# Moving the small product of the softmax sums and their reciprocals from VectorE to GpSimd

## The reference, cut to what matters

```python
def attention(x, w_in, b_in, w_out, b_out):          # x: 8 x 512 x 256, 16 heads of 16
    x_proj = (x @ w_in.T + b_in).reshape(b, l, h, -1)
    q, k, v = jnp.split(x_proj, 3, axis=-1)
    att = jnp.einsum('blhd,bmhd->blmh', q, k) * scale
    att = jax.nn.softmax(att, axis=2)
    opt = jnp.einsum('blmh,blhd->blhd', att, v).reshape(b, l, d)
    return opt @ w_out.T + b_out

x = x + layernorm(attention(layernorm(x)))
x = x + layernorm(feed_forward(layernorm(x)))
```

## Time and profile before

| | |
|---|---|
| median of three runs | 537.91 us (537.71 to 538.23) |
| the profiled execution's own time | 539.01 us |
| its span, first to last instruction | 537.2 us |
| PE busy | 512.8 us (95%) |
| DVE busy | 473.9 us (88%) |
| ACT busy | 453.8 us (84%) |
| POOL busy | 344.9 us (64%) |
| granted TensorE clock, mean | 0.997 of full speed |

### The profile page before, as it was taken

One profiled execution on the slowest core, in us unless ns is written; L12 is line 12 of the kernel. 1 busy time (PEld: TensorE's weight loads), 2 busy tenths in 40 slices (PEclk: granted clock), 3 DMA queues, 4 the chain that ended last, 5 costly groups with the idle time before them and its releaser, 6 DMA issues.

```text
span 537.2 us, 8929 instructions
## 1 busy us (share of the span) xinstructions
PE 512.8 (95%) x2752; PEld 410.2 (76%) x2752; DVE 473.9 (88%) x1005; ACT 453.8 (84%) x1238; POOL 344.9 (64%) x544
## 2 busy tenths in 40 slices
PE   8999989999999999999999999999999999999995
PEld 6746555688898769876897779876897777678995
DVE  4598999988999899998999899999999899995455
ACT  3599998999899998999899998999899988895230
POOL 5697047415973788539972798449971888497462
PEclk9999999999999999999999999999999999999998
DMA  6694353026220635036230625035310760210011
GB/s 215 205 224 131 95 142 78 2 51 168 53 82 2 157 80 156 2 78 158 60 99 1 163 74 157 1 97 138 80 39 6 177 171 1 65 54 1 1 40 40
DMA packets 22691, 47.63 MB, mean 89 GB/s; under 512 B 5266, under 2 KB 13586, under 8 KB 22004
## 3 DMA queue, kind: packets, MB, share of 16 engines
q1 hardware_dynamic: 21956, 45.95, 32.5%
q10 hardware_dynamic: 432, 0.59, 0.4%
q0 software_dynamic: 256, 0.52, 0.4%
HBM read 8.24 MB, written 4.19 MB: 23 GB/s over the span
## 4 chain that ended last, share of the span: by engine, by line
PE 42%; ACT 35%; DVE 9%; SPq 4%; issue 3%; POOL 3%; DMA 1%; POOLq 0%; ACTq 0%
ACT ps L523 26%; PE pu L199 20%; PE ps L227 8%; PE pu L283 4%; PE ps L199 3%; DVE nmax L735 3%; SPq L1199 3%; ACT qk L537 3%; PE pu L239 2%; PE ps L206 2%; DVE st L777 2%; ACT y L590 2%; DMA stack<-qk 1%; ACT vo L545 1%; POOL y L1029 1%
## 5 line engine op out<-in xcount | busy, mean ns | idle before, releaser
L523 ACT ACTIVATE ps<-ps,nmax 128x512 f32<-128x512 f32 x512 | 348.9, 721 | 19.2 <-DVE nmax L735 18.3
L735 DVE TENSOR_REDUCE nmax<-ps 128x1 f32<-128x512 f32 x512 | 322.3, 680 | 17.4 <-PE ps L227 16.8
L227 PE MATMUL ps<-stack 128*128 128x512 f32 x512 | 184.6, 418 | 3.9 <-ACT ps L523 3.2
L523 ACT ACTIVATION_READ_ACCUMULATOR ps<-ps,nmax 128x1 f32 x512 | 137.6, 269 | 0.0
L227 PEld LDWEIGHTS ps<-stack 128*128 128x128 f32 x512 | 93.5, 189 | 33.5 <-ACT ps L523 20.9
L199 PEld LDWEIGHTS pu<-wo_r,inter 128*128 128x128 f32 x696 | 88.3, 188 | 2.8
L199 PE MATMUL pu<-wo_r,inter 128*128 128x256 f32 x696 | 90.4, 282 | 0.0
L199 PE MATMUL pu<-yT,wi_r 128*128 128x512 f32 x336 | 87.4, 395 | 0.4 <-ACT xn L590 0.4
L199 PEld LDWEIGHTS pu<-yT,wi_r 128*128 128x128 f32 x336 | 63.1, 189 | 14.1 <-ACT xn L590 0.7
L206 PE MATMUL ps<-ones_r 128*128 128x512 f32 x132 | 55.3, 461 | 6.2 <-ACT ps L523 5.1
L206 PEld LDWEIGHTS ps<-ones_r 128*128 128x128 f32 x132 | 25.9, 199 | 32.4 <-ACT ps L523 26.2
(11 more groups left out here) (154 smaller groups left out, 701.5 us busy)
## 6 DMA issues: line engine op xcount, KB each, us to landing
stack<-qk SPq DMA_DIRECT2D x256, 128.0 KB, 2.5
xb<-in_x SPq DMA_DIRECT2D x7, 512.0 KB, 3.7
out_y<-xb SPq DMA_DIRECT2D x7, 512.0 KB, 3.6
xb<-in_wo SPq DMA_DIRECT2D x1, 1024.0 KB, 7.8
vo<-in_wi SPq DMA_DIRECT2D x2, 512.0 KB, 7.0
oT<-in_wqk ACTq DMA_DIRECT2D x1, 512.0 KB, 4.9
xb<-in_x SPq DMA_DIRECT2D x4, 128.0 KB, 4.8
stack<-qk SPq DMA_DIRECT2D x8, 64.0 KB, 2.5
```

What stands on the lines that cost most here:

```text
L227: e.matmul(ps[i % NS][:], st[:, 1 - p, c, t * 128:(t + 1) * 128], st[:, 2, c, :], start=True, stop=True).then_inc(scored, 1)
L523: e.activation(ps[i % NS][:], ps[i % NS][:], ACT.Exp, bias=nmax[:, i % 8:i % 8 + 1], accum_out=ssum[:, b % 2, t, h:h + 1]).then_inc(exped, 1)
L735: e.tensor_reduce(nmax[:, i % 8:i % 8 + 1], ps[i % NS][:], AX_X, ALU.max, negate=True).then_inc(maxed, 1)
```

## The change

The product that makes `sone` is taken out of VectorE's `ratio` and `ratio_half` and put at the head of GpSimd's `scale` and `scale_half`, behind their waits. VectorE now signals a new semaphore `inverted` after the reciprocal, GpSimd waits for it, multiplies, signals `ratioed` and waits for its own signal before it scales. The counts of `ratioed` are halved where they are waited for.

```diff
@@ scalar, exponential @@
                 if b >= 2 and k == 0:
-                    e.wait_ge(ratioed, 2 * (b - 2) + 2)
+                    e.wait_ge(ratioed, b - 1)
@@ vector, ratio @@
                     if b:
                         e.wait_ge(scaled, 4 * b)
-                    e.reciprocal(srec[:], ssum[:, b % 2]).then_inc(ratioed, 1)
-                    e.wait_ge(ratioed, 2 * b + 1)
-                    e.tensor_tensor(sone[:], ssum[:, b % 2], srec[:], ALU.mult).then_inc(ratioed, 1)
+                    e.reciprocal(srec[:], ssum[:, b % 2]).then_inc(inverted, 1)
@@ vector, ratio_half @@
-                e.reciprocal(srec[:, ts], ssum[:, b % 2, ts]).then_inc(ratioed, 1)
-                e.wait_ge(ratioed, 2 * (b + h) + 1)
-                e.tensor_tensor(sone[:, ts], ssum[:, b % 2, ts], srec[:, ts], ALU.mult).then_inc(ratioed, 1)
+                e.reciprocal(srec[:, ts], ssum[:, b % 2, ts]).then_inc(inverted, 1)
@@ pool, scale @@
                     e.wait_ge(v_whole, 4 * b + 4)
-                    e.wait_ge(ratioed, 2 * b + 2)
+                    if b:
+                        e.wait_ge(scaled, 4 * b)
+                    e.wait_ge(inverted, b + 1)
+                    e.tensor_tensor(sone[:], ssum[:, b % 2], srec[:], ALU.mult).then_inc(ratioed, 1)
+                    e.wait_ge(ratioed, b + 1)
                     scale_tiles(b, ALL)
@@ pool, scale_half @@
-                e.wait_ge(ratioed, 2 * (b + h) + 2)
+                ts = slice(2 * h, 2 * h + 2)
+                e.wait_ge(scaled, 4 * b)
+                e.wait_ge(inverted, b + h + 1)
+                e.tensor_tensor(sone[:, ts], ssum[:, b % 2, ts], srec[:, ts], ALU.mult).then_inc(ratioed, 1)
+                e.wait_ge(ratioed, b + h + 1)
                 scale_tiles(b, HALVES[h])
```

More of the change, by code:

```diff
@@ L117, in sandwich @@
         scored, maxed, exped = sem("scored"), sem("maxed"), sem("exped")
-        ratioed, scaled = sem("ratioed"), sem("scaled")
+        inverted, ratioed, scaled = sem("inverted"), sem("ratioed"), sem("scaled")
         xnT_ps, qk_ps, v_ps, oT_ps, y_ps, yT_ps = (sem(n + "_ps") for n in ("xnT", "qk", "v", "oT", "y", "yT"))
```

## The result

Over 15 runs each, the changed kernel takes 536.75 us (536.47 to 538.28) and the kernel before 537.81 us: a ratio of 0.9983, with a 95% interval of 0.9976 to 0.9990. That is 0.9 to 1.1 us less, where the prediction said 0.4 less and a range of 535.2 to 538.8. The verdict "same", which the prediction drew at 0.2% or 1.08 us, holds, by the medians with 0.02 us to spare. But the interval doesn't reach 1: it is a small gain, and more than twice the size that was forecast.

A forecast was written before the change was run, and what follows sets the result against it. The period was taken to close over GpSimd (ScalarE, copy, subtraction, scaling, transposes, projection), with the held product beside it. The terms sum to 7p - 2.73 = -0.4 us, from 537.91 to 537.5 us, range 535.2 to 538.8.

The forecast's parts named there:

- The hold: VectorE's product at five changes of sequence waits about 1.5 us until GpSimd's long subtraction ends; it is not slow itself.
- The chain's 1.35 us: "Issue" time of VectorE's product in the chain of waits; claimed no measure of gain, as the period closes over GpSimd.
- VectorE is the bound: Rival: VectorE sets the pace, so five holds of 1.64 us go: -8.2 us, 529.7 us; chance 0.08.
- both of TensorE's waits go: Rival: at four steady changes TensorE's waits of 0.41 and 0.27 us vanish: -2.7 us, 535.2 us; chance 0.10.
- The four steady changes: Changes near 191, 250.8, 310.6 and 370.4 us: scaling later, second transposes no longer wait; p - 0.50 each.
- p: Time of the product on GpSimd, taken as 0.33 us from a plain two-input operation of 128 x 64.
- d: How much later GpSimd's scaling starts at a steady change: p - 0.07, or 0.26 us.
- The seventh change: Change into the last sequence: ScalarE's copy, late before from VectorE's stall, then follows the transposes; p - 0.35.
- The first change and the last half: Places without a hold, where TensorE waits for the scaling, so its delay is paid: p - 0.19 each.
- The second change: Scaling ends at 135.50, TensorE needs it at 136.10; 0.46 us cover the delay, so it costs nothing.
- The queue behind the product: GpSimd's later copy, subtraction and norms, delayed 0.26 us, hidden by TensorE's work; uncovered, 1.0 us over four periods.
- The slower rival: Product dear on GpSimd, delaying each handover to TensorE: slower by 1.08 us from p = 0.54; chance 0.12.

The follow-up runs named there:

- e1: Changed kernel plus a spare VectorE product of the reciprocals that nobody reads, not in the last sequence's halves: 537.84 us against 537.41 for the kernel before, ratio 1.0011.
- e6: Kernel before, product on VectorE, with GpSimd's scaling moved between its copy and the long subtraction: 539.20 us against 537.51, ratio 1.0030.
- e7: Kernel before with GpSimd's subtraction ahead of the scaling split into two of 128 x 512: 534.79 us in one execution against 537.51.
- e9: Changed kernel with the product back on VectorE at the first change and in the last sequence's halves: 536.06 us against 537.63 for the kernel before, ratio 0.9971.
- e2: Changed kernel with GpSimd making the product twice, the second behind its own signal: 539.05 us, ratio 1.0035 to the kernel before.
- e5: Changed kernel with GpSimd's product and scaling moved between its copy and the long subtraction: 540.28 us against 537.51 for the kernel before, ratio 1.0051.
- e10: Changed kernel with GpSimd making the product six times at the first change, lengthening TensorE's wait: 540.11 us against 537.48 for the kernel before, ratio 1.0053.
- e11: Changed kernel with six products at the first change and TensorE's wait filled with twelve matmuls of ones: 538.24 us against 537.48 for the kernel before, ratio 1.0014.
- e4: Kernel before with VectorE making the product two maxima later, except at the first change and in the halves: 535.44 us against 537.41, ratio 0.9964.
- e7b: Kernel before with GpSimd's subtraction ahead of the scaling split in two, timed over 5 runs: 534.98 us against 537.63, ratio 0.9950.
- e8: Kernel before with VectorE's product two maxima later and GpSimd's copy and subtraction done alternately by halves: 534.26 us against 537.63, ratio 0.9939.

## Why the prediction was right, and where it was off

*The hold.* Right, and shown from three sides: e1 (a product that nobody needs is held as long), e6 (0.22 us with no subtraction beside it), e7 (the hold ends with the half). The Trainium skill (SBUF — State Buffer, section "Who interferes with whom") says that a VectorE instruction with two SBUF inputs contends with a GpSimd instruction that reads SBUF, and that whoever issues first keeps the shared ports for its whole instruction. All three runs agree.

*The chain's 1.35 us are not the price.* Right. The loop closes over GpSimd, and VectorE touches it at the second transposes alone. With the hold gone a period fell by 0.28 us, not by 1.35 or 1.64. The rivals in which VectorE is the bound, or in which both of TensorE's waits go, are refuted by the 0.55 us that are left of the first and the 0.64 us at L802.

*The four steady changes, p - 0.50 each.* The form was right, the constant mis-sized. Forecast -0.17 us each with p = 0.33; measured 239.10 us before and 237.96 in the changed kernel from the second change's projection to the sixth's, -0.285 each, with p = 0.32. The step that failed is "a dependent pair on GpSimd has 0.08 us between them", which I put on both sides of the product. It holds behind it (192.24 to 192.32), where the scaling waits for the product's signal. Ahead of it nothing is waited for, since the reciprocal is long done, and the product starts 0.04 us before the subtraction's recorded end. So d was 0.13 us and not 0.26, and the constant is 0.62. The signs that hang on d were off by the same amount: TensorE's first wait is 0.55 us and not 0.67, and the period is 0.28 us shorter and not 0.17. The trace of before held this too: the copy behind the four scalings, with its wait met, starts at 195.24, and they end at 195.29.

*The seventh change, p - 0.35.* The same 0.12 us: forecast -0.02, measured -0.14 (59.65 to 59.51 us from the sixth projection).

*The first change and the last half, p - 0.19 each.* Right: +0.14 us at either, and e9 gives both back. Here the product does wait for a signal.

*The second change.* 0.03 us less, forecast nothing: covered, as said. In the changed kernel the scaling ends there at 134.91 (132.54 + 2.37) and TensorE starts at 135.35; less the 0.14 us for the signal, 0.30 us of the cover are left, and the doubled product of e2, 0.40 us longer, costs 0.1 us at this change.

*The queue behind the product, costed at nothing.* Right. In the changed kernel GpSimd's norm ends at 215.81 (214.71 + 1.10) and TensorE starts its transposes at 216.14, with no wait. But the cover is smaller than it was, 0.33 us in place of 0.85: the projection now comes earlier in the period, and GpSimd's work behind the product later. In e5 the cover is gone, and TensorE waits there.

*The sum.* From the distances in the traces the terms are 0.14 - 0.03 - 4 x 0.285 - 0.14 + 0.14 = -1.03 us. Two stretches that no term covers are longer, by 0.05 us (from the seventh change's projection to the last half's reciprocal) and 0.08 us (behind the last projection); why is open. So from the first reciprocal to the end the changed kernel takes 0.90 us less, where the ratio gives 0.9, the medians 1.06, and the forecast was 0.4. The wrong gap enters at five places, the four steady changes and the seventh: 5 x 0.12 = 0.6 us, about the size of the miss. With it and p = 0.32 the prediction's sum is -1.09 us.

*The margins.* 536.75 us lies in the range of 535.2 to 538.8, but not in the 536.9 to 538.3 that were given for the forecast alone. That the gain stayed under the 1.08 us where the prediction drew its line between same and faster, with 0.02 us to spare, owes something to luck.

*p.* 0.32 us for a forecast 0.33. The factor of the Trainium skill's GPSIMD Engine Reference (section "Performance versus the Vector engine", 1.96 for an addition of two inputs, measured at 2048 elements) would have given 0.44, an estimate. For 128 x 64 the traces give 0.323 over 0.225, 1.44.

*The slower rival.* Its mechanism is real, as e2 shows, and p stayed under its threshold. (Its price at p = 0.70 is too low by 0.17 us: by the prediction's own cover of 0.46 us, d would be paid at the second change too.) What I had not listed is a second way to be slower: the added 0.14 us at the first change lengthen a wait of TensorE from 1.41 to 1.57 us, and in 2 of 15 runs the changed kernel ran 1.5 us longer at a lower mean clock. That the clock falls behind a wait at this place is shown by e10 and e11. That those two runs were such falls is argued from their clock and time, since neither was profiled.

*Open.* Why 2 of 15 runs with the wait of 1.57 us, 3 of 11 with 1.55 us (e1) and 1 of 5 with 1.95 us (e2) stand out and not all, no run here tells. Of these six only one, of e1, was profiled, and the mean clock of the runs of e1 and e2, 0.996 to 0.998, is no lower than that of ordinary runs. A run can also stand 0.6 us above the others with no fall behind this wait: the profiled one of e5, with a wait of 1.56 us and a clock of 1.00 there. Kernels with the first change as before (e4, e6, e7b, e8, e9, and the kernel before) showed no such runs.

## What to carry to other kernels

When an instruction on VectorE with two SBUF inputs takes far longer than its shortest, look at what GpSimd ran at its end; shift either in time, or split the long one, before giving work to the slower engine: the move gained 0.17%, a shift of two maxima 0.36%, the split alone 0.50%, and shift, split and filling together 0.61%. Don't price a wait by its length in the chain; follow what the next consumers wait for second, here a bank and the projection behind it. And take the gap between two instructions from a pair of the same kind, in its instructions and in its wait, met or unmet: 0.12 us at each of five places was most of this miss.

## What the hardware showed that I had not expected

At this place the gap between two GpSimd instructions is 0.07 to 0.08 us where the second waits for the first's signal, and none where its waits are already met. That is not so for every pair: in the changed kernel's trace the small TENSOR_SCALAR of 128 x 4 at 198.21 starts 0.09 us behind a subtraction, though its input has been ready for some 5 us, and the next one, at 198.53, 0.08 us behind it, though it waits for nothing.

```profile
198.21 0.24 POOL L1016 TENSOR_SCALAR nmr<-mv 128x4 f32<-128x4 f32 x1
198.53 0.24 POOL L1017 TENSOR_SCALAR nmr<-mv 128x4 f32<-128x4 f32 x1
```

What makes the difference there is open. And a wait of TensorE of about 1.6 us at this place passes in most runs but perhaps not in all: the granted clock was 0.53 for 3.4 us behind a wait of 1.55 us in one profile, and 1.00 throughout behind one of 1.57 in another.
